# Second norm's statistics from an accumulated Gram matrix of the queries, in place of a first pass of all output products

## The reference

```python
t = _to_tokens(x)                                   # (4, 4096, 128)
# _L1_attn_ref(_ln_t(t), ...), per image, h = 4 heads of d = 32
q = softmax(q, axis=2) * scale                      # over the 32 entries of a head
k = softmax(k, axis=3)                              # over the tokens
context = einsum('bhcj,bhdj->bhcd', k, v)
out = einsum('bhcd,bhdi->bhci', context, q)
out = W_out @ out + b_out
mean = jnp.mean(out, axis=(1, 2), keepdims=True)    # one mean per image
var = jnp.var(out, axis=(1, 2), keepdims=True)      # one variance per image
out = (out - mean) * rsqrt(var + 1e-5) * gn_w + gn_b
t = t + out
```

## Time and profile before

| | us |
|---|---|
| median of 3 runs | 3012.91 |
| lowest, highest | 3011.15, 3014.59 |
| the profiled execution, device time | 3014.32 |
| the profiled execution, span of the trace | 3012.5 |
| busy PE, DVE, ACT, POOL | 2864.8, 2538.3, 2409.8, 709.7 |

### The profile page before, as it was taken

How to read it: one execution, slowest core, us unless ns; L and a number is a source line. 1 busy time by engine, 2 the same in 40 slices (tenths; PEclk the granted TensorE clock), 3 DMA queues, 4 the chain that set the end, 5 groups by cost and what they waited for, 6 DMA issues and landing times.

```text
span 3012.5 us, 52105 instructions
## 1 busy us (share of the span) xinstructions
PE 2864.8 (95%) x20254; PEld 972.6 (32%) x20254; DVE 2538.3 (84%) x3559; ACT 2409.8 (80%) x3137; POOL 709.7 (24%) x726
## 2 busy tenths in 40 slices
PE   6999999988899999998889999999988999999988
PEld 3222222275422222227432222223843222222373
DVE  5888989877888888887788888898778888888877
ACT  4999999943799999975479999997448999999744
POOL 1122222213412222211432221212153222122115
PEclk9999999998999999999899999999989999999998
DMA  2555555500165555550026555555002655555400
GB/s 82 113 111 111 111 110 111 113 7 15 57 119 106 113 112 112 109 103 1 14 73 114 112 111 112 109 103 99 1 21 55 114 108 113 111 99 112 85 1 28
DMA packets 72078, 257.00 MB, mean 85 GB/s; under 512 B 8160, under 2 KB 10240, under 8 KB 71808
## 3 DMA queue, kind: packets, MB, share of 16 engines
q0 software_dynamic: 64512, 234.91, 41.2%
q1 hardware_dynamic: 7296, 18.51, 1.7%
HBM read 10.12 MB, written 8.39 MB: 6 GB/s over the span
## 4 chain that ended last, share of the span: by engine, by line
PE 87%; ACT 6%; DVE 5%; issue 1%; POOL 1%; DMA 0%; SPq 0%; POOLq 0%; DVEq 0%; ACTq 0%
PE BK L1106 85%; ACT EA L559 2%; ACT KE L559 2%; PE BK L1111 1%; DVE ST L673 1%; POOL KE L484 1%; ACT KE L576 1%; ACT K L613 1%; ACT SMC L548 0%; DVE X L921 0%; DVE X L1084 0%; DVE RU L667 0%; DVE RU L666 0%; PE BK L1456 0%; DMA WEXP<-in_L_ffn_expert_w 0%
## 5 line engine op out<-in xcount | busy, mean ns | idle before, releaser
L883 DVE TENSOR_TENSOR XT<-XT,KE 128x512 f32<-128x512 f32 x1344 | 1573.5, 1229 | 150.2 <-ACT KE L559 148.2
L559 ACT ACTIVATE KE<-BK 128x512 f32<-128x512 f32 (+1 forms) x1536 | 1490.4, 1022 | 129.1 <-PE BK L1106 34.3
L1106 PE MATMUL BK<-Q,K 32*128 32x512 f32 x8192 | 1168.6, 640 | 18.5 <-ACT KE L559 12.2
L1106 PE MATMUL BK<-KE,V 128*32 128x512 f32 x6144 | 815.8, 604 | 5.2 <-ACT SMC L548 5.2
L443 POOL DMA_DIRECT2D RM<-EA x448 | 392.7, 958 | 1511.7 <-ACT EA L559 686.9
L1106 PEld LDWEIGHTS BK<-Q,K 32*128 32x128 f32 x8192 | 320.0, 183 | 875.5 <-ACT KE L559 626.2
L559 ACT ACTIVATE EA<-BK 128x512 f32<-128x512 f32 (+1 forms) x512 | 497.4, 1025 | 28.8 <-PE BK L1106 1.9
L1106 PEld LDWEIGHTS BK<-KE,V 128*32 128x32 f32 x6144 | 125.4, 108 | 583.4 <-issue 533.8
L1106 PE MATMUL BK<-EA,V 128*32 128x512 f32 x2048 | 272.6, 604 | 0.0
L641 ACT ACTIVATE RM<-BK,GT 128x128 f32<-128x128 f32 x512 | 145.5, 371 | 133.1 <-PE BK L1106 122.8
L1106 PE MATMUL BK<-WEXP,XT 128*128 128x512 f32 x512 | 238.6, 614 | 9.3 <-DVE X L1084 9.3
(11 more groups left out here) (179 smaller groups left out, 1738.7 us busy)
## 6 DMA issues: line engine op xcount, KB each, us to landing
RM<-EA POOLq DMA_DIRECT2D x224, 768.0 KB, 6.7
RM<-EA POOLq DMA_DIRECT2D x224, 256.0 KB, 3.3
XN<-in_x SPq DMA_DIRECT2D x16, 512.0 KB, 5.7
out<-X SPq DMA_DIRECT2D x16, 512.0 KB, 2.6
WEXP<-in_L_ffn_expert_w SPq DMA_DIRECT2D x1, 512.0 KB, 6.6
CONST<-in_consts SPq DMA_DIRECT2D x1, 384.0 KB, 5.7
WQKV<-in_L_conv_w_qkv SPq DMA_DIRECT2D x1, 192.0 KB, 2.3
WQKV<-in_L_attn_W_qkv SPq DMA_DIRECT2D x1, 192.0 KB, 5.8
```

The lines of the kernel that those rows point to most:

```text
L559: nc.scalar.activation(exps(jt, p), scored(c * T + jt, p).rearrange("p a n -> p (a n)"), ACT.Exp, scale=SCALE0).then_inc(s_exp, 1)
L883: v.tensor_tensor(acc, acc, exps(jt, p), ALU.add).then_inc(s_adds, 1)
L1106: return nc.tensor.matmul(o, lhsT, rhs, start=start, stop=stop, skip_group_check=shared)
```

## The change

The sum and the sum of squares of Y = Qe AT follow from the 128x128 matrix M = Qe^T Qe, the sum over all tokens of the outer product of a token's query with itself. Each row of Qe sums to 4 (before the scale), so the row sums of M are 4 times the column sums of Qe. The changed kernel therefore:

- has PE accumulate M over 32 tiles in BK[7][:, 0:128] (`gram`), with a tile of QE as both the weights and the moving operand, in place of the first pass of 32 products;
- moves the transposes of QE behind that (`turn`), into BK[1] to BK[6] in turn, in pairs with small products between them;
- has DVE copy M (GS), sum its rows, and scale two constant matrices by these sums (MQ, MA); PE multiplies both by AT, which gives the mean's rows and so ATC = AT - mean; PE multiplies GS by ATC; DVE multiplies by ATC and sums; PE averages over partitions; the rest (inverse square root, GA, GB, AT2) is as before, with one more addition;
- puts all four `residual` products ahead of `second`, in the order 3, 1, 2, 0.

GS, MQ, MA, ATC and WV (the last product) lie in a part of the buffer KE that is free by then. The core of the diff:

```diff
-MIX_LINKS = 115
+MIX_LINKS = 117
+        GS, MQ, MA, ATC, WV = (KE[:, 2 * N + i * C:2 * N + (i + 1) * C] for i in range(5))
-        OPENED = 3
+        TURNS = 6
+        def turn_bank(i):
+            return BK[1 + i % TURNS]
 # ACT
                 for i, c in enumerate(q_order):
                     act.wait_ge(s_qT, b * NCH + i + 1)
-                    nc.scalar.activation(QT[:, c * CH:(c + 1) * CH], BK[c], ACT.Copy).then_inc(s_qTc, 1)
+                    nc.scalar.activation(QT[:, c * CH:(c + 1) * CH], turn_bank(i), ACT.Copy).then_inc(s_qTc, 1)
 # DVE
-                for i, c in enumerate(q_order):
-                    dve.wait_ge(s_y1, b * NCH + i + 1)
-                    last = v.bn_stats(ST[:, c, :], BK[c])
-                mix_link(last)
+                dve.wait_ge(s_gram, b + 1)
+                mix_link(v.tensor_copy(GS, BK[7][:, 0:C]))
+                mix_link(v.reduce_sum(SMALL[:, 1:2], GS, X_AX))
+                v.tensor_scalar(MQ, BLOCK, SMALL[:, 1:2], 1.0 / (SCALE1 * H * N), ALU.mult, ALU.mult)
+                v.tensor_scalar(MA, ONES, SMALL[:, 1:2], 1.0 / (H * N), ALU.mult, ALU.mult).then_inc(s_bst, 1)
+                dve.wait_ge(s_gst, b * 3 + 1)
+                v.tensor_tensor(ATC, AT[:, :], BK[0][:, 2 * C:3 * C], ALU.subtract).then_inc(s_bst, 1)
+                mix_link(v.bn_stats(ST[:, 0, :], BK[0][:, 3 * C:4 * C]))
                 settle(dve)
-                v.bn_aggr(MV[:, :], ST[:, 0:NCH, :].rearrange("p a s -> p (a s)")).then_inc(s_bst, 1)
-                ... (mean and second moment through PE, two waits on s_gst)
+                v.bn_aggr(MV[:, :], ST[:, 0, :]).then_inc(s_bst, 1)
+                dve.wait_ge(s_bst, b * 4 + 3)
+                v.tensor_scalar(SMALL[:, 0:1], MV[:, 0:1], -1.0, None, ALU.mult)
+                dve.wait_ge(s_gst, b * 3 + 2)
+                mix_link(v.tensor_tensor(WV, ATC, BK[7][:, C:2 * C], ALU.mult))
+                v.reduce_sum(SMALL[:, 2:3], WV, X_AX).then_inc(s_bst, 1)
+                dve.wait_ge(s_gst, b * 3 + 3)
+                mix_link(v.tensor_scalar(RA[:, 0:1], BK[7][:, 0:1], -1.0 / N, 1e-5, ALU.mult, ALU.add))
+                mix_link(v.tensor_tensor(RA[:, 0:1], RA[:, 0:1], MV[:, 1:2], ALU.add))
                 rsqrt(mix_link, SMALL[:, 3:4], RA[:, 0:1], 1)
 # PE: the lines L1367 to L1389 are replaced by
+                def gram(i):
+                    pe.wait_ge(s_q1n, b * NCH + i + 1)
+                    c = q_order[i]
+                    for t in range(c * TPB, (c + 1) * TPB):
+                        last = mm(BK[7][:, 0:C], QE[:, t * P:(t + 1) * P], QE[:, t * P:(t + 1) * P],
+                                  start=(t == q_order[0] * TPB), stop=(t == (q_order[-1] + 1) * TPB - 1))
+                    return last
+                def turn(i):
+                    if i >= TURNS:
+                        pe.wait_ge(s_qTc, b * NCH + i - TURNS + 1)
+                    transposes(turn_bank(i), lambda t: QE[:, t * P:(t + 1) * P], q_order[i]).then_inc(s_qT, 1)
+                pe.wait_ge(s_q1s, b * NCH + NCH)
+                for i in range(NCH):
+                    if i == 4:
+                        pe.wait_ge(s_at, b * 3 + 1)
+                        mm(BK[0][:, C:2 * C], CTX[:, :], WOUT1[:, :]).then_inc(s_ctx, 1)
+                    last = gram(i)
+                    if i == NCH - 1:
+                        last.then_inc(s_gram, 1)
+                turn(0)
+                turn(1)
+                pe.wait_ge(s_at, b * 3 + 2)
+                pe.wait_ge(s_bst, b * 4 + 1)
+                mm(BK[0][:, 2 * C:3 * C], MQ, AT[:, :])
+                mm(BK[0][:, 3 * C:4 * C], MA, AT[:, :]).then_inc(s_gst, 1)
+                turn(2)
+                turn(3)
+                pe.wait_ge(s_bst, b * 4 + 2)
+                mm(BK[7][:, C:2 * C], GS, ATC).then_inc(s_gst, 1)
+                turn(4)
+                turn(5)
+                pe.wait_ge(s_bst, b * 4 + 4)
+                mm(BK[7][:, 0:1], NEG, SMALL[:, 2:3]).then_inc(s_gst, 1)
+                turn(6)
+                turn(7)
+                pe.wait_ge(s_qTc, b * NCH + 3)
+                residual(3)
+                pe.wait_ge(s_qTc, b * NCH + 7)
+                residual(1)
+                pe.wait_ge(s_qTc, b * NCH + NCH)
+                residual(2)
+                pe.wait_ge(s_bst, b * 4 + 3)
+                residual(0)
                 pe.wait_ge(s_at, b * 3 + 3)
                 def second(c):
-                    if OPENED <= c < HCH:
-                        residual(c)
```

More of the change, by code:

```diff
@@ L295, in hybrid_kernel @@
         s_qTc = sem("s_qTc")
-        s_y1 = sem("s_y1")
+        s_gram = sem("s_gram")
         s_y2 = sem("s_y2")
@@ L988, in _ @@
                 mix_link(v.memset(G32[:, :, :], 0.0))
-                for i, c in enumerate(q_order):
-                    dve.wait_ge(s_y1, b * NCH + i + 1)
-                    last = v.bn_stats(ST[:, c, :], BK[c])
-                mix_link(last)
-                settle(dve)
-                v.bn_aggr(MV[:, :], ST[:, 0:NCH, :].rearrange("p a s -> p (a s)")).then_inc(s_bst, 1)
[L996 to L1002, removed]
+                dve.wait_ge(s_gram, b + 1)
[6 more added lines that the diff above has]
+                mix_link(v.bn_stats(ST[:, 0, :], BK[0][:, 3 * C:4 * C]))
+                settle(dve)
+                v.bn_aggr(MV[:, :], ST[:, 0, :]).then_inc(s_bst, 1)
[7 more added lines that the diff above has]
+                mix_link(v.tensor_tensor(RA[:, 0:1], RA[:, 0:1], MV[:, 1:2], ALU.add))
                 rsqrt(mix_link, SMALL[:, 3:4], RA[:, 0:1], 1)
```

## The result

The changed kernel takes 2989.59 us (median of 4 runs, 2986.01 to 2994.89), against 3012.4 us of the kernel before (4 runs). The ratio is 0.9925, 95% interval 0.9913 to 0.9937. Measured once more later (last experiment) it was 0.9943, 0.9931 to 0.9955. The forecast was 2991, range 2984 to 3001, faster.

A forecast was written before the change was run, and what follows sets the result against it. Up to second, PE and then a serial DVE/PE chain bound the stage, then PE alone until logits. Starting second 4.55 us earlier and shortening it by 0.86 gives 5.4 per batch, 21.6 in all: 2991 us, range 2984 to 3001.

The forecast's parts named there:

- The gram pass: PE's 64 gram records replace the first pass, start at 656.10 without POOL holding PE, and end at 663.63.
- rival 4: In gram, load and stream of one block can't overlap: 12.3 us more per batch, 3040 in all; chance 4%.
- The serial chain: DVE and PE steps behind gram, 0.29 us per new 128-column DVE instruction; AT2 ready at 671.64.
- Rival 2: Engine handovers in the statistics chain bite: AT2 at 673, later than PE; gain 4.5 per batch, 2995; chance 10%.
- PE late by 0.4 us: Ahead of second, PE's residual products end after AT2, so second begins at 672.1 in place of 676.66.
- The residual product: residual(3) leaves second, taking 0.86 us from everything behind it, counted in full until logits at 698.96.
- The stage's sum: Earlier second (4.55 us) and shorter second (0.86 us): together 5.4 us per batch, 21.6 us over four batches.
- The clock: Turns and small products, 663.6 to 668.7, keep 2.4 GHz; the half-clock stretch of 672.1 to 675.6 goes.
- rival 1: The clock falls among the turns: gain 3.65 per batch, 2998, at worst 1.0 and 3009; chance 12%.
- rival 3: The later half-clock stretch, 702.9 to 720.0, lies otherwise: 2998 if longer, 2984 if shorter; 8% for a clear loss.

The follow-up runs named there:

- experiment 3: Changed kernel with all transposes first, then the whole gram pass, then small and residual products with no turn between; 3014.04 us, ratio 1.0.
- experiment 4: Changed kernel with all eight chunks of transposes ahead of the small products, none between; 2992.12 us, ratio 0.9938.
- experiment 11: As experiment 8, with DVE's row sums of M read straight from PSUM ahead of the copy GS; 2973.08 us, ratio 0.9867.
- experiment 1: Kernel before, with all four residual products ahead of the second pass and none inside it; 3011.72 us, ratio 0.9995.
- experiment 2: Changed kernel with residual(3) back inside the second pass, ahead of chunk 3; 2985.83 us, ratio 0.991.
- experiment 7: Changed kernel with 30 unread products of constants on PE while DVE chooses the experts; 2989.93 us, ratio 0.9922.
- experiment 8: As experiment 7, plus 12 such products ahead of layer 1's first transposes and 8 behind the first bias product; 2975.48 us, ratio 0.9881.
- experiment 9: As experiment 7, with 60 transposes of a constant block in place of the 30 products; 2995.45 us in one execution.
- experiment 10: As experiment 7, with 28 products of eight columns in place of the 30 products; 3007.68 us in one execution.
- experiment 6: Kernel before, with eight dependent one-column DVE instructions more ahead of GA; 3022.8 us, ratio 1.0032.

## Why the prediction was right, point by point

The stage came as worked out wherever the clock stayed at 1.00. What the prediction left out are the clock's falls elsewhere, and that the time came so near is in part luck (the last point).

- **The gram pass.** Predicted end 663.63, in the changed trace 656.27 + 3.74 + 3.62 = 663.63. The cost of a record is 0.112 us with one block in both roles, so rival 4 is refuted by the trace itself.
- **The serial chain.** 0.29 us for each new DVE instruction was right to 0.01. Each of the three round trips came where it was put; AT2 was predicted at 671.64 and came at 668.01 + 3.62 = 671.63. Rival 2 did not occur. Experiments 3 and 4 show what carried it: the chain's length is 1.5 us worse than before, and the transposes inside it are worth 1.4 us against having them in front.
- **PE late by 0.4 us.** Predicted `second` at 672.1, measured 668.46 + 3.62 = 672.08. Of this, 0.29 us is what PE's lateness costs: by so much AT2 to logits is shorter in experiment 4, where PE waits for AT2. Experiment 11 agrees: the first small product 0.32 us earlier moved both AT2 and `second`.
- **The residual product.** 0.86 us inside `second`, predicted `second` to `logits` 21.4, measured 689.89 - 668.46 = 21.43. That it is the change's gain needs a reservation from experiment 1: the kernel before could have had it where its clock did not fall.
- **The stage's sum.** Predicted 5.4 us per batch, 21.6 in all. Where the clock stays at 1.00 it is 4.39 + 1.07 = 5.46, in the first batch 4.51 + 0.93 = 5.44; four such batches would be 21.8. The two profiles have 16.6 and 11.3. The step that did not hold is the one by which PE runs from AT2 to `logits` at full rate in all four batches alike, so that the gain arrives whole: the falls in the routing took back 5.2 and 10.5 us.
- **The clock.** The half-clock stretch behind the idle chain went, as predicted, and rival 1 did not occur: 659.8 to 665.0 at 1.00. In the nine profiles with the changed order of PE (the changed kernel twice, experiments 2, 4 and 7 to 11) the clock fell between CTX and AT2 in none of 36 batches; in those of the kernel before and of experiments 3 and 6 it fell in all twelve. But it fell in none of the four of experiment 1, whose chain has the same idle time, so idle time there allows the fall and does not force it. Experiment 9 shows transposes by themselves keeping the clock. The Trainium skill's sentence (TensorE: Matmul & The Clock Gate, Part 4: PE-mode transpose), by which the full clock doesn't engage for transposes, does not hold here by these rows.
- **What was left out, and the luck.** Everything outside the stage was taken as unchanged but for rival 3, and rival 3 had one place where there are three. The expert section is shorter by 1.4 to 1.8 us, with 6.5 to 9.8 us at half clock behind GT in place of 12.2 to 12.5. The section before CTX, in the later batches, varies by 0.9 us for each 3.4 us of half clock. The routing, which I had as PE at full rate, lost 0.7 to 0.8 or 3.4 to 3.7 us where the clock fell. Experiment 6 moves these without the change, and experiment 8 takes most of them away. Experiment 10 shows that products of eight columns alone do not keep the clock, which points at those of the routing; why it falls there in some batches and not in others of one kernel is not shown. In the first profile the sections outside the stage gave 12.0 us and the routing took 5.2, which makes a gain of 6.8 over the stage's 21.8 (28.6 of the span); in the second it was 8.7 and 10.5, a loss of 1.8 (20.0). So the forecast's nearness owes something to two omissions of opposite sign. Taken over all ten executions of both sets the median is 2992.7 us, and the first median is 3 us below it.

Left open: why before's batches all lie alike. They are 743.8 to 744.1 us apart and their falls stand at nearly the same places in each; the changed kernel's batches of 736 to 741 us do not. That batch length decides this was not tested.

## What to carry to other kernels

Replacing a statistics pass by an algebraic identity pays here only through the order that it allows: look for what it frees from a dependence, and put the freed work into the gaps of the new serial chain. For edits worth under 0.2%, compare the stage's own instants in two traces, since the clock's falls elsewhere move the total by more. When PE's idle holes are filled to keep its clock, fill all of them (2975 us), because one alone (2990 us) gave nothing here: the clock fell in the next hole, and where it had fallen before, the added products themselves held PE up by 2.0 to 2.4 us.

## What was not expected of the hardware

- PE fell to 1.2 GHz while busy without a break, behind stretches with many products of eight columns: the routing (672.0 to 679.5, and 2885.7 to 2889.1) and experiment 10. Transposes of 128 columns did not do this (experiment 9, one execution).
- The same idle 2.4 us cost the clock in one execution and not in another of nearly the same kernel (experiment 1), and single executions of that kernel differ by 13 us (3001.3 to 3014.8), with a mean granted clock of 0.987 and 0.980. Of the 13.0 us by which the profiled one's span is below before's, 5.4 lie in the stage.
- Filling idle stretches with products that nobody reads makes the changed kernel 0.4 to 0.6% faster (0.9881 against 0.9925 and 0.9943 of before), though it adds PE work (2975.5 us).
